# Products six and seven of a Strassen step as pairs of 64-row matmuls: one kernel on one Trainium2 core

## The reference

```
x = x + einsum('bct,bcd->bdt', x, L0[cond])                 # 64x64 mixing over tokens
x = x + einsum('bct,bcd->bdt', x, L1[cond])                 # again
x = x + (x W^T + 0.5 * (x A[label]) B^T)                    # dense 1024x1024, with a low-rank part of rank 32
x = x + einsum('bsi,boi->bso', x, L3[adapter])              # one of 8 dense 1024x1024 matrices per batch
```

## Time and profile before

| | |
|---|---|
| median of 3 runs | 384.58 us (383.71 to 386.38) |
| the profiled execution, span from first to last instruction | 383.7 us |
| PE busy | 376.3 us, 98% of the span, 1733 matmuls |
| PEld busy | 313.1 us, 82% |
| DVE, ACT, POOL busy | 267.6, 225.1, 117.2 us |
| TensorE's granted clock, mean | 0.999 |

### The profile page before, as it was taken

How to read it: one execution, slowest core, us unless ns; L and a number is a source line. 1 busy time by engine, 2 the same in 40 slices (tenths; PEclk the granted TensorE clock), 3 DMA queues, 4 the chain that set the end, 5 groups by cost and what they waited for, 6 DMA issues and landing times.

```text
span 383.7 us, 7652 instructions
## 1 busy us (share of the span) xinstructions
PE 376.3 (98%) x1733; PEld 313.1 (82%) x1734; DVE 267.6 (70%) x301; ACT 225.1 (59%) x299; POOL 117.2 (31%) x157
## 2 busy tenths in 40 slices
PE   8999999999999999999989999999999999999995
PEld 7888888888888888888868888888888888888784
DVE  4786978847849788446967367864589635999653
ACT  4679577587247375254475365843577536779443
POOL 0000231000000000024856337654177532676600
PEclk9999999999999999999999999999999999999999
DMA  8975905630277294406527106562256622565223
GB/s 293 398 266 202 347 0 196 224 129 16 97 281 280 97 328 165 164 3 220 170 91 240 44 23 192 209 174 59 56 172 216 168 58 58 195 202 158 60 62 86
DMA packets 24187, 61.38 MB, mean 160 GB/s; under 512 B 1906, under 2 KB 2098, under 8 KB 24114
## 3 DMA queue, kind: packets, MB, share of 16 engines
q1 hardware_dynamic: 23648, 60.10, 46.7%
q10 hardware_dynamic: 466, 0.44, 0.4%
HBM read 52.15 MB, written 8.39 MB: 158 GB/s over the span
## 4 chain that ended last, share of the span: by engine, by line
PE 93%; DMA 2%; DVE 1%; POOL 1%; ACT 1%; ACTq 1%; issue 1%; POOLq 0%; SPq 0%
PE ps L1514 40%; PE ps L1373 12%; PE ps L1374 12%; PE ps L1375 12%; PE ps L1400 4%; PE ps L1537 4%; PE ps L1439 3%; PE ps L1602 2%; PE ps L1412 2%; DMA raw<-w3t 2%; DVE ring L1266 1%; PE ps L1552 1%; POOL st L490 0%; ACT L662 0%; POOL st L492 0%
## 5 line engine op out<-in xcount | busy, mean ns | idle before, releaser
L1514 PE MATMUL ps<-ring,aT 128*128 x752 | 173.4, 390 | 0.0
L1514 PEld LDWEIGHTS ps<-ring,aT 128*128 128x128 f32 x752 | 141.0, 188 | 29.8 <-issue 0.7
L1373 PE MATMUL ps<-ring 128*128 128x512 f32 x208 | 81.1, 390 | 0.0
L1374 PE MATMUL ps<-ring 128*128 128x512 f32 x208 | 81.0, 389 | 0.0
L1375 PE MATMUL ps<-ring 128*128 128x512 f32 x208 | 81.0, 389 | 0.0
L476 POOL TENSOR_TENSOR aT<-xT,aT 128x512 fp32r<-128x512 f32 (+1 forms) x36 | 56.8, 1598 | 48.4 <-ACT aT L761 44.2
L1266 DVE TENSOR_TENSOR ring<-raw,ring 128x1024 f32 (+1 forms) x40 | 62.8, 1628 | 5.9 <-ACT ring L747 5.9
L767 ACT ACTIVATE aT<-ps 64x1024 fp32r<-64x1024 f32 x32 | 32.7, 1020 | 49.2 <-PE ps L1514 48.8
L1294 DVE TENSOR_TENSOR stage<-ps,stage 64x1024 f32<-64x1024 f32 x30 | 36.7, 1222 | 28.1 <-ACT stage L776 27.5
L1283 DVE TENSOR_TENSOR aT<-ps,aT 64x1024 fp32r<-64x1024 f32 x32 | 39.1, 1222 | 23.7 <-ACT aT L767 23.1
L1375 PEld LDWEIGHTS ps<-ring 128*128 128x128 f32 x208 | 39.0, 188 | 8.1
(11 more groups left out here) (95 smaller groups left out, 329.5 us busy)
## 6 DMA issues: line engine op xcount, KB each, us to landing
raw<-w3t SPq DMA_DIRECT2D x40, 512.0 KB, 4.5
ring_f<-xt SPq DMA_DIRECT2D x8, 1024.0 KB, 7.9
raw<-xt SPq DMA_DIRECT2D x8, 1024.0 KB, 5.2
out<-stage SPq DMA_DIRECT2D x30, 256.0 KB, 3.1
ring_f<-wt SPq DMA_DIRECT2D x4, 1024.0 KB, 8.1
xT<-xt SPq DMA_DIRECT2D x3, 1024.0 KB, 10.5
xT<-wt SPq DMA_DIRECT2D x2, 1024.0 KB, 16.3
ring_f<-wt SPq DMA_DIRECT2D x4, 256.0 KB, 4.4
```

The lines of the kernel that those rows point to most:

```text
L1373: pe.matmul(dst, hi_of(qw)[:, k, cs], hi_of(qx)[:, k, :], start=start and k == 0, stop=False, skip_group_check=True)
L1374: pe.matmul(dst, hi_of(qw)[:, k, cs], lo_of(qx)[:, k, :], start=False, stop=False, skip_group_check=True)
L1514: last = pe.matmul(acc(i)[:, n, :], x3_split(i, k, start, P), ring[:, bass.ds(off + (part * D + n * 512), 512)], start=(k == 0 and j == 0) ...
```

## The change

P6 and P7 of both `j` are done by a new function `by_rows` in place of `product`. It splits each contraction tile of 128 rows into its upper and its lower 64 rows. Matmuls come in pairs: one takes 64 rows for one output tile, the next takes the other 64 rows for another output tile. Four turns, `TURNS`, go over the tiles: upper rows of tile 0 with lower rows of tile 1, then upper of 2 with lower of 3, then upper of 1 with lower of 0, then upper of 3 with lower of 2. So each product has 96 matmuls of 64 rows in place of 48 of 128, each with its own weight load. A tile's two halves are added in its bank, the second two turns after the first; the third and fourth turns wait on a new semaphore `rows` which the first and second raise at their ends. `l2` is raised in the third turn for tiles 0 and 1 and in the fourth for tiles 2 and 3. The waits for the seed and for `u2` stand at the heads of the first and second turns, for both tiles of the turn.

```
+            ROWS = (slice(0, T), slice(T, P))
+            TURNS = ((0, 1), (2, 3), (1, 0), (3, 2))
+            turned = [0]
+
+            def by_rows(w, n, dst_of, start, stop, ready):
+
+                qw, qx = w_slot(w), x_slot(n)
+                passes = ((hi_of(qw), hi_of(qx)), (hi_of(qw), lo_of(qx)), (lo_of(qw), hi_of(qx)))
+                for turn, os in enumerate(TURNS):
+                    if turn < 2:
+                        ready(min(os)), ready(max(os))
+                    else:
+                        pe.wait_ge(s("rows"), turned[0] + 2 * (turn - 1))
+                    for k in range(HALF):
+                        if turn == 0:
+                            pe.wait_ge(s("w_lo"), HALF * w + (k // 2 + 1) * 2)
+                            pe.wait_ge(s("x_lo"), HALF * n + (k // 2 + 1) * 2)
+                        for i, (a, b) in enumerate(passes):
+                            begins, ends = turn < 2 and k == 0 and i == 0, k == HALF - 1 and i == 2
+                            for o in sorted(os):
+                                half = ROWS[os.index(o)]
+                                last = pe.matmul(dst_of(o), a[half, k, P * o:P * (o + 1)], b[half, k, :],
+                                                 start=start and begins, stop=stop and ends and turn >= 2,
+                                                 skip_group_check=True)
+                                if ends:
+                                    last.then_inc(s("rows" if turn < 2 else "l2"), 1)
+                turned[0] += HALF
+
+            def product_by_rows(w, n, phase, j, start, stop, ready):
+
+                by_rows(w, n, lambda o: ps_l2(phase, j, o), start, stop,
+                        lambda o: pe.wait_ge(s(ready), HALF * j + o + 1))
...
-                product(2, 4 + 3 * j, 1, j, False, True, "seed")
-                product(3, 5 + 3 * j, 1, j, False, True, "u2")
+                product_by_rows(2, 4 + 3 * j, 1, j, False, True, "seed")
+                product_by_rows(3, 5 + 3 * j, 1, j, False, True, "u2")
```

## The result

The changed kernel takes 385.65 us (median of 20 runs, 385.15 to 387.34) against 384.07 us for the one before in the same series (20 runs, 383.06 to 386.38). The ratio is 1.0045, with a 95% interval of 1.0033 to 1.0057: 1.7 us slower, 1.3 to 2.2 (the two medians are 1.6 us apart). The forecast was 385.4 us and "within 1%", that is, a change of +0.86 us.

What follows compares the result with a forecast made beforehand. It took PE, busy 98% of the span, as the bound: pairs at 0 plus 0.86 us for mode changes on 384.58 gave 385.4 us, range 382.4 to 389.0, with 0.82 for within 1%.

Steps and rivals of the forecast that it cites:

- PE is the path and changes count one to one: Around P6, P7 and C21 PE has no slack, so each ns gained or lost there reaches the end.
- Pairs run side by side, at the price of one 128-row matmul: In P6 and P7 a pair of 64-row matmuls takes 227 ns, like one 128-row matmul: 192 x 0 = 0.
- Rival (c): Pairs in P6 and P7 don't overlap and take up to 454 ns: +43.5 us, 429 us; chance 0.10.
- 4 ns per pair: From the Trainium skill: each further packed tile adds about 4 ns; if not overlapped between pairs, 0.8 us more over 192.
- The surcharge of 13 ns stays: In P6 and P7 the 13.3 to 14 ns over the bare stream stays for pairs, as a limit on reading columns.
- Rival (a): The surcharge goes away in pairs, 213.3 to 216 ns each: gain 2.1 to 2.6 us less 0.86, 383.1; chance 0.22.
- Rival (b): Two loads per pair cost more than one, pairs of 230 to 245 ns: 386 to 389 us; chance 0.14.
- Changes of mode: Passing between 128-row and 64-row matmuls around P6 and P7: 0.23 us in, 0.20 out, twice, 0.86 in all.
- Twice the instructions, the waits, the releases at nothing: Doubled instructions, the `rows` wait and moved releases of `u2` and `u3` cost nothing; `u3` of tile 2 holds by 0.8 us.
- The base: The profiled execution spans 383.7 us; the median of the runs is 0.9 above it, so the forecast adds to 384.58.
- Same row by row, shifted: Outside the change, the profile after should show the rest of the kernel the same row by row, only shifted.

Runs made afterwards that it cites:

- second profile of before: The kernel before, unaltered, run again against itself: ratio 0.9985 (0.9973 to 0.9998), with no waits of PE after C12.
- order-only kernel: Kernel before with whole 128-row matmuls in P6 and P7, tiles 0 and 1 in turn, then 2 and 3, no 64-row matmul: ratio 0.9996.
- P6 alone: P6 by 64-row pairs, P7 by 128-row matmuls, against the kernel before: ratio 1.0074 (1.0044 to 1.0103), +2.8 us.
- j = 0 alone: P6 and P7 by 64-row pairs for the first `j` only, against the kernel before: ratio 1.0062 (1.0037 to 1.0087), +2.4 us.
- extra matmul: The full change plus one unused 128-row matmul between P6 and P7 of each `j`, against the kernel before: ratio 1.0094, +3.6 us.

## Why the prediction was right

The time, 385.65 against 385.4, and the ratio lie where they were forecast. That the times agree to 0.25 us is in part luck. The forecast added 0.86 us to 384.58, the median of three runs, which lies 0.5 us above the 384.07 that 20 runs give. The change itself was measured at 1.7 us (1.3 to 2.2), about twice the 0.86, which lies outside that interval. What the forecast did get right is the cost on PE's path, 0.98.

- **PE is the path and changes count one to one.** Right up to C12: the path grew by 0.98 us, and nothing between hid it. The argument for the part behind it misread a row: PE does not stand still from 183 to 200 us. It runs 72 matmuls from 182.44 on (the row above) and waits once, for the 1.64 us before 200.56; the chain leaves PE there only because it is followed back from that wait. The wait is absent in the second profile of before and in both of the changed kernel. So after C12 a difference on PE is carried on only as far as such waits let it.
- **Pairs run side by side, at the price of one 128-row matmul.** Right: 96 pairs in 21.76 us, 226.7 ns, beside 226.7 for 128 rows. Taken away, with the same rows for both, the path went up by 39.0 us. Rival (c) is out for this shape. The 4 ns per pair for which the prediction gave a price of 0.8 us are not there either: 96 pairs are 21.76 us without them.
- **The surcharge of 13 ns stays.** Right: a pair takes 227 ns, and one 64-row matmul alone takes 227 too. Rival (a) is out. Rival (b) as well: two loads per pair cost nothing. The argument for it was not borne out. It put the 13 ns down to reading columns at full speed, but they are the same at 256 and at 512 columns, which the prediction's own rows showed (120 and 227 ns), so they are no limit on reading. Nor does bf16, at 216 ns, rule out the load, which is shorter there as well. Why an fp32r matmul costs 13 ns more than its stream, and why two side by side pay this once, stays open.
- **Changes of mode.** Forecast 0.23 in and 0.20 out, 0.86 in all; measured 0.25 and 0.24, 0.98 in all. The size was a little short because the matmuls after the first one on the way out are also longer by some ns each, which the term left out. The prediction feared that the 0.35 us of idle time at line 1449 was a wait for the mixing tables. The new way in has the same 0.35 <-issue, with no tables to wait for.
- **Twice the instructions, the waits, the releases at nothing.** Right: the order-only kernel has the path and time of before, and the tightest wait, `u3` of tile 2, was met (copy at 86.84, PE without a wait).
- **The base.** The prediction put the profiled execution 0.9 us below the median. That compared a span with device times. The profile after has both, a span of 384.2 us and a time of 385.96: 1.8 us apart. The profiled execution of before was therefore about 385.5 us (an estimate), 1.4 us above the median and not level with the fastest run; 1.64 us of it is the wait near 200 us. The forecast against the median did not use it.
- **Same row by row, shifted.** Not so: the part after C12 differed by up to 2 us between profiles of one kernel.

What stays open: the timed difference of the change is 0.3 to 0.7 us above the path's 0.98, that of P6 alone and of j = 0 alone 1.9 us above theirs, and that of the extra matmul 1.3. Neither the length of the code nor the lateness of PE seems to account for it. That it is waits of PE in the slots is what the profiles suggest, and was not shown for the timed runs.

## What to carry to other kernels

If the contraction fills 128 rows, splitting it into row groups that run side by side gains nothing: a pair costs what the whole cost, and each passage between 128 and 64 rows adds a quarter of a us on a saturated PE, so 64-row work belongs together in as few blocks as possible. Before trying to hide a small surcharge behind a neighbour, compare it at two numbers of columns: one that doesn't grow with them is a price per matmul, and what pays it has to be found by changing one operand at a time. Here overlap did not remove it. For differences well under 1%, compare the distance between two rows of PE's own chain, which repeats to 0.01 us here, and run the kernel against itself.

## What the runs showed of the hardware

- A change between 128-row and 64-row matmuls costs PE 0.25 us on the way in and 0.24 on the way out, with 512 columns and a granted clock of 1.00; the changed kernel (two profiles), P6 alone and `j` = 0 alone agree to 0.01 us.
- Two fp32r matmuls of 64 rows and 512 columns in different row groups and banks run in 227 ns together, and one such matmul alone takes 227 too. Two in the same row group take 227 each, also in different banks.
- With a load each time, an fp32r matmul of 512 columns takes 227 ns and one of 256 columns 120: 13 ns over the bare stream in both. A bf16 one of 512 columns takes 216, with a load of 98 ns in place of 187.
- A plain float32 matmul shows as two records, each of twice the stream (430 ns for 512 columns), and records in different row groups run side by side.
